# A block-sparse convolution's fourth tap stage, summed on GpSimd by additions instead of on TensorE by one-hot products

## The chip, the cores and the metric
The kernel runs on one core of one Trainium2 chip. The metric is the device time of one execution in microseconds; lower is better. A core has TensorE (PE in the profile; PEld is its weight load), VectorE (DVE), ScalarE (ACT), GpSimd (POOL) and SyncE (SP), which here only issues DMAs. GpSimd issues DMAs too, from its own instruction stream.

## What is computed
Four blocks in a row, each with a residual and a layer norm ahead of it, in float32 on an input of 2 x 512 x 256: a block-sparse convolution, a mixture of experts, an attention and the same mixture of experts again. Only the convolution is touched:

```
def _L0_attn_a_ref(x, block_values, cols, rows):      # x: (2, 512, 256), block_values: (128, 64, 64, 16)
    xb = x.reshape(batch, n_block_row, bs, t)          # 8 channel blocks of 64
    x_unfold = xb[:, cols].reshape(batch, n_blocks * bs, t)
    W = block_values.reshape(n_blocks * bs, bs, ks)
    o = jax.lax.conv_general_dilated(x_unfold, W, window_strides=(1,), padding=[(ks - 1, 0)],
            dimension_numbers=('NCH', 'OIH', 'NCH'), feature_group_count=n_blocks)
    y = jnp.zeros(...).at[:, rows].add(o.reshape(batch, n_blocks, bs, t))
    return y.reshape(batch, n_block_row * bs, t)

x = x + _L0_attn_a_ref(_layernorm(x), block_values, cols, rows)
x = x + _L0_ffn_ref(_layernorm(x), ...)
x = x + _L0_attn_b_ref(_layernorm(x), ...)
x = x + _L0_ffn_ref(_layernorm(x), ...)
```

128 weight blocks of 64 x 64 with 16 taps each (33.5 MB) are read. Blocks with the same pair (column, row) act on the same input and output channels, so the kernel first sums the weights of equal pairs (64 pairs are possible, and in this input only 16 low pairs carry weights: column and row numbers are below 4), and then multiplies the sums with the input.

## The kernel before
The 16 taps are split in eight stages of two taps. The two taps and the 64 input channels fill the 128 partitions. A stage's weights are summed over equal pairs in one of two ways.

**One-hot stages (0 to 4, `NPE = 5`).** Their weights arrive in banks, `wconv`, 512 KB each, eight for each stage, issued by SP (L247) into a ring of `RING = 6` buffers; a buffer is free again when its bank is summed (`summed`). TensorE sums a bank with the one-hot matrix of the pairs: `sum_bank`, L534, eight products with a moving size of 64, which the trace shows as 16 matmuls, as each float32 product takes two. Four PSUM banks are used in turn. ACT evicts each of them in `round_banks` (L285 for the high pairs into `full`, L286 the rounded low pairs), DVE takes the low part (`low_banks`, L397), and `sum_bank` waits for the low part of four banks earlier.

**Added stages (5 to 7, `ND = 3`).** Their weights arrive by block: `wtaps`, 16 chunks of eight blocks, 768 KB each, issued by GpSimd (L348) into three buffers `raw_d`. Before the load of chunk d (d >= 3) GpSimd waits until DVE has added chunk d - 3. DVE adds each block to the running sum `acc` of its pair, at an address from a register, in two halves (`add_block`, L421, 128 x 96: three stages of 32 columns). The pair numbers are loaded into DVE's registers eight at a time (`load_pairs`). An addition waits for all but the one before it. The additions are placed between the low parts of the banks by the table `BANK_BLOCKS`: five blocks after each bank of stages 2 and 3, then six. So DVE's order is one list: a low part that stands behind an addition waits for it.

**Products.** `products` (L545) multiplies the sums of one pair of rows with the input in three float32r products (high x high, low x high, high x low), 24 for each stage over the eight `LOW_PAIRS`. In `sum_and_convolve` the products of stage st - 1 stand between the banks of stage st, by `PACE`. `finish_products` (L568) ends a stage and raises `ws_free`, which starts at 2. `convolve_last_banks` multiplies the last one-hot stage. Then `convolve_added` multiplies the added stages, first all for row group 0, then for row group 1, after ACT (`round_sums`, L290) and DVE (`low_sums`, L405) have rounded them. ACT starts that after `ws_free` at `NPE + 1`, which is the end of stage 3's products, and after all additions. The transposes of the next layer norm (L129) stand ahead of the last piece. The first matmuls of the mixture of experts (L1131) follow the convolution's last product.

GpSimd has nothing between its loads but their waits; behind them it has a small subtraction (L157) and the powers of the next layer norm (L90).

Of the kernel before, what the change touches and what calls it, by code (L numbers as in the profile page):

```python
# [29 lines left out]
XPITCH = 272  # L30
NPE, ND = 5, 3
OB, DB, RING = 8, 8, 6

# [128 lines left out]
def conv_phase(nc, cm, pm, ps, ins, following, prefetch, first_weights):  # L162


    with ExitStack() as ctx:
        sb = lambda n, s, d: ctx.enter_context(nc.sbuf_tensor(f"cv_{n}", s, d))
        NW = NCB * NCB
        CHUNK = OB * P
        DROW = ND * BS
        NDC = NBLK // DB  # L170
# [9 lines left out]
                         .rearrange("p (w o) -> p w o", w=NLOW) for i in range(2)] for part in range(2))  # L180
        ws_hi += [sb(f"ws_hi{i}", [P, NLOW, BS], F32R)[:] for i in range(2, ND + 1)]
        ws_lo += [sb(f"ws_lo{i}", [P, NLOW, BS], F32R)[:] for i in range(2, ND + 1)]
        full = [sb(f"full{i}", [P, NW - NLOW, BS], F32) for i in range(2)]
        acc = sb("acc", [P, ND, NW, BS], F32)
        colrow = sb("colrow", [P, 2], I32)
        colrow_f = sb("colrow_f", [P, 2], F32)
# [15 lines left out]
            "zeros_ready", "ones_ready", "cr_in", "line_in", "iota_done", "const_done",  # L202
            "cr_conv", "pair_part", "pair_ready", "onehot_ready", "acc_zeroed", "added",
            "count_ready", "flag_ready", "stats_done", "moments_done", "var_ready", "rstd_ready", "xn_ready",
# [13 lines left out]
        FIRST_BLOCKS = 14  # L218
        BANK_BLOCKS = ((5,) * 8, (5,) * 8, (6, 6, 6, 6, 6, 4, 0, 0))
        PACE = (0, 0, 2, 2, 4, 4, 6, 8)  # L220
# [6 lines left out]
        def slot_of(st):  # L227
            return st % 2 if st <= NPE else st - NPE + 1

# [3 lines left out]
        def piece_of(st, r):  # L233
            return NPE * SB + r * ND + (st - NPE)

# [33 lines left out]
        def scalar(a):  # L269

            def round_input(i):
                if i == 0:
                    a.wait_ge(s["pads_ready"], 2)
                a.wait_ge(s["xn_ready"], GC * (i // 4 + 1))
                dst, src = copies(i)
                a.activation(dst(xc_hi), src, ACT.Copy).then_inc(s["xc_hi_done"], 1)

            def round_banks(st, banks=range(SB)):
                slot = st % 2
                if 0 in banks:  # L280
                    a.wait_ge(s["ws_free"], st + 1)
                for q in banks:
                    a.wait_ge(s["summed"], st * SB + q + 1)
                    sums, cols = ps[q % BANKS][:].rearrange("p (w o) -> p w o", o=OB), slice(q * OB, (q + 1) * OB)
                    a.activation(full[slot][:, :, cols], sums[:, NLOW:NW, :], ACT.Copy)  # L285
                    a.activation(ws_hi[slot][:, :, cols], sums[:, 0:NLOW, :], ACT.Copy).then_inc(s["ws_hi_done"], 1)  # L286

            def round_sums(st, r):
                e = st - NPE
                a.activation(row_part(ws_hi[slot_of(st)], r), row_part(acc[:, e, 0:NLOW, :], r), ACT.Copy)\  # L290
                 .then_inc(s["ws_hi_done"], 1)

            a.wait_ge(s["ones_ready"], 1)
            a.activation(spare[:], ones[:], ACT.Copy)
            round_banks(0, range(0, 5))
            for i in range(3):
                round_banks(0, range(5 + i, 6 + i))
                round_input(i)
            for i in range(3, 8):
                round_banks(1, range(i - 3, i - 2))  # L300
                round_input(i)
            round_banks(1, range(5, 8))
            for st in range(2, NPE):
                round_banks(st)
            a.wait_ge(s["ws_free"], NPE + 1)
            a.wait_ge(s["added"], 2 + 2 * NBLK)
            for r in range(GC // 2):
                for st in range(NPE, NST):
                    round_sums(st, r)
            first_weights["round"](a)  # L310
            a.activation(spare[:], ones[:], ACT.Silu)

        def gpsimd(g):
# [27 lines left out]
            clear_sums(range(3, ZEROED))  # L341
            g.wait_ge(s["rstd_ready"], B)
            for d in range(NDC):
                if d in (1, 2):
                    g.wait_ge(s["xc_lo_done"], 4 * d)
                if d >= 3:
                    g.wait_ge(s["added"], 2 + 2 * DB * (d - 2))
                g.dma_start(raw_d[d % 3], ins["wtaps"][d].rearrange("p (n f) -> p n f", n=DB)).then_inc(raw_d_in[d % 3], 16)  # L348
            first_weights["low"](g)
# [25 lines left out]
        def vector(v):  # L375
# [26 lines left out]
            def low_sums(st, r):  # L402
                e = st - NPE
                v.wait_ge(s["ws_hi_done"], piece_of(st, r) + 1)
                v.tensor_tensor(row_part(ws_lo[slot_of(st)], r), row_part(acc[:, e, 0:NLOW, :], r),  # L405
                                row_part(ws_hi[slot_of(st)].bitcast(F32), r), ALU.subtract).then_inc(s["ws_lo_done"], 1)
# [6 lines left out]
            def add_block(i, pairs):  # L413
                d, n = divmod(i, DB)
                if n == 0:
                    v.wait_ge(raw_d_in[d % 3], 16 * (d // 3 + 1))
                for k in range(2):
                    part = slice(k * BS // 2, (k + 1) * BS // 2)
                    dst = acc[:, :, bass.ds(pairs[n], 1), part].rearrange("p e a f -> p e (a f)")
                    src = raw_d[d % 3][:, n, :].rearrange("p (e f) -> p e f", e=ND)[:, :, part]  # L420
                    add = v.tensor_tensor(dst, dst, src, ALU.add)  # L421
                    add._wait_ge(s["added"], i * 2 + k + 1)
                    add.then_inc(s["added"], 1)
# [66 lines left out]
            for st in range(2, NPE):  # L490
                for q in range(SB):
                    low_banks(st, range(q, q + 1))
                    end = done + BANK_BLOCKS[st - 2][q]
                    edge = -(-done // DB) * DB
                    more = load_pairs(edge // DB) if edge < end else pairs
                    for i in range(done, end):
                        add_block(i, pairs if i < edge else more)
                    done, pairs = end, more
            for r in range(GC // 2):
                for st in range(NPE, NST):  # L500
                    low_sums(st, r)
# [9 lines left out]
        def tensor(t):  # L511
# [37 lines left out]
            def high_products(st):  # L549

                for c in range(NCB):
                    for r in range(GC):
                        if c >= NCB // 2 or r >= GC // 2:
# [3 lines left out]
                            else:  # L557
                                sums = acc[:, e, w:w + 2, :]
                            for x in (xc_hi, xc_lo):
# [26 lines left out]
            def convolve_added():  # L586
                for st in range(NPE, NST):
                    t.wait_ge(s["ws_lo_done"], piece_of(st, 0) + 1)
                    with t.If(flag != 0):
                        t.wait_ge(s["added"], 2 + 2 * NBLK)  # L590
                        high_products(st)
                    if st == NST - 1:
# [1440 lines left out]
```

## Time and profile before

| | us |
|---|---|
| median of 3 runs | 873.85 |
| lowest, highest | 873.17, 874.07 |
| span of the profiled execution, first to last instruction | 873.0 |
| TensorE busy, of the span | 865.5 |
| DVE busy | 501.8 |
| ACT busy | 420.0 |
| GpSimd busy | 320.0 |

The convolution takes the first 126 us of the span; the rest is the mixture of experts, the attention and the mixture of experts again. The profile counts an instruction as busy from its start to its end; matmuls overlap each other, so the mean duration of one is longer than the distance from one to the next. The chain of waits merges neighbouring instructions of one line into a piece with its start, its length and their count. The DMA share is that of the core's 16 DMA engines. "Idle before" names what released an engine that had waited; "issue" is time for which no wait is shown.

### The profile page before, as it was taken

The numbers are of one execution on the slowest core, as the hardware profiler recorded it, in microseconds if no ns is written. First come the engines' busy times: TensorE is split into PE (matmuls) and PEld (weight loads), VectorE is DVE, ScalarE is ACT, GpSimd is POOL, SyncE is SP. The second block draws the span as 40 slices with busy tenths as digits, with TensorE's granted clock in tenths as the row PEclk, the third lists the DMA queues.
The fourth block names the chain that finished last, engine by engine and source line by source line (L and its number), as shares of the span: only waits on it lengthen the run. The fifth ranks groups of instructions, "written<-read, shape, count | busy, mean of one in ns | idle before, by whom it ended". The sixth has DMA issues, their size and how long they took to land.

```text
span 873.0 us, 16737 instructions
## 1 busy us (share of the span) xinstructions
PE 865.5 (99%) x5617; PEld 773.3 (89%) x5620; DVE 501.8 (57%) x1360; ACT 420.0 (48%) x978; POOL 320.0 (37%) x293
## 2 busy tenths in 40 slices
PE   9999999999999999999999999999999999999998
PEld 7999878888888888889989998998997888888887
DVE  4777757333333338887688668768877433333334
ACT  3522416334334344776377557647746433434332
POOL 5211014556555564232121213212112556556552
PEclk9999999999999999999999999999999999999999
DMA  8999312111111102000000100000002111111111
GB/s 338 362 383 391 136 40 77 49 54 36 54 45 45 54 18 76 1 26 21 18 3 21 36 0 24 0 0 1 1 1 73 38 54 39 51 54 36 54 36 49
DMA packets 25554, 61.01 MB, mean 70 GB/s; under 512 B 3298, under 2 KB 10916, under 8 KB 25508
## 3 DMA queue, kind: packets, MB, share of 16 engines
q1 hardware_dynamic: 23204, 47.82, 16.1%
q0 software_dynamic: 2304, 12.58, 3.8%
q8 instruction: 28, 0.46, 0.2%
q14 instruction: 18, 0.15, 0.0%
HBM read 59.35 MB, written 1.05 MB: 69 GB/s over the span
## 4 chain that ended last, share of the span: by engine, by line
PE 93%; DVE 3%; ACT 1%; DMA 1%; issue 1%; POOL 0%; DVEq 0%; ACTq 0%
PE bank L1131 29%; PE bank L1655 25%; PE bank L1144 14%; PE bank L534 7%; PE bank L545 5%; PE bank L1781 4%; PE bank L1721 3%; PE bank L1157 2%; PE bank L1167 2%; DMA cv_shared<-in_wtaps 1%; PE bank L1746 1%; DVE cv_acc L421 1%; PE bank L518 1%; PE bank L1675 1%; PE bank L129 0%
## 5 line engine op out<-in xcount | busy, mean ns | idle before, releaser
L1030 DVE TENSOR_TENSOR f_h<-f_scaled,bank 128x512 f32<-128x512 f32 (+1 forms) x90 | 60.8, 676 | 179.4 <-POOL f_scaled L895 166.9
L812 ACT ACTIVATE f_h_hi<-f_h 128x512 fp32r<-128x512 f32 (+2 forms) x102 | 63.6, 624 | 186.2 <-DVE f_h L1030 186.0
L895 POOL TENSOR_TENSOR f_scaled<-f_act,f_gate_rows 128x512 f32<-128x512 f32 x80 | 102.9, 1287 | 116.3 <-ACT f_act L805 115.9
L1131 PE MATMUL bank<-f_xt_hi,f_w_lo 128*128 128x512 f32 x352 | 138.2, 393 | 0.0
L1131 PE MATMUL bank<-f_xt_hi,f_w_hi 128*128 128x512 f32 x352 | 137.8, 391 | 0.0
L1350 ACT ACTIVATE at_prob<-bank,at_sbias,at_qrs 128x512 f32<-128x512 f32 (+3 forms) x128 | 77.6, 618 | 72.6 <-DVE at_sbias L1542 72.6
L1037 DVE TENSOR_TENSOR f_h_lo<-f_h,f_h_hi 128x512 fp32r<-128x512 f32 (+2 forms) x102 | 71.8, 704 | 70.7 <-ACT f_h_hi L812 70.4
L1131 PE MATMUL bank<-f_xt_lo,f_w_hi 128*128 128x512 f32 x352 | 108.8, 390 | 0.0
L1144 PE MATMUL bank<-f_w_lo,f_h_hi 128*128 128x256 f32 (+1 forms) x352 | 99.6, 283 | 0.0
L1144 PE MATMUL bank<-f_w_hi,f_h_lo 128*128 128x256 f32 (+1 forms) x352 | 99.6, 283 | 0.0
L1144 PE MATMUL bank<-f_w_hi,f_h_hi 128*128 128x256 f32 (+1 forms) x352 | 99.3, 282 | 0.0
L805 ACT ACTIVATE f_act<-bank 128x512 f32<-128x512 f32 (+2 forms) x102 | 59.9, 589 | 52.6 <-PE bank L1131 46.4
L1413 POOL TENSOR_TENSOR at_qrs<-at_qsum,minus_half 128x4 f32<-128x4 f32 x32 | 32.8, 1025 | 137.7 <-DVE at_qsum L1503 137.7
L1131 PEld LDWEIGHTS bank<-f_xt_lo,f_w_hi 128*128 128x128 f32 x352 | 66.1, 188 | 14.4
L1131 PEld LDWEIGHTS bank<-f_xt_hi,f_w_lo 128*128 128x128 f32 x352 | 66.4, 189 | 11.1
L1131 PEld LDWEIGHTS bank<-f_xt_hi,f_w_hi 128*128 128x128 f32 x352 | 66.5, 189 | 11.0
L1144 PEld LDWEIGHTS bank<-f_w_hi,f_h_lo 128*128 128x128 f32 (+1 forms) x352 | 67.2, 191 | 3.4
L1144 PEld LDWEIGHTS bank<-f_w_hi,f_h_hi 128*128 128x128 f32 (+1 forms) x352 | 67.2, 191 | 3.3
L884 POOL TENSOR_TENSOR f_w_lo<-f_wraw,f_w_hi 128x512 fp32r<-128x512 f32 x46 | 59.5, 1293 | 25.3 <-ACT f_w_hi L791 25.3
L1144 PEld LDWEIGHTS bank<-f_w_lo,f_h_hi 128*128 128x128 f32 (+1 forms) x352 | 67.2, 191 | 0.0
L1538 DVE TENSOR_REDUCE at_smax<-bank 128x1 f32<-128x512 f32 (+3 forms) x128 | 58.8, 485 | 2.3 <-PE bank L1655 2.0
L889 POOL TENSOR_TENSOR f_w_lo<-f_wraw,f_w_hi 128x256 fp32r<-128x256 f32 x46 | 43.9, 954 | 35.1 <-ACT f_w_hi L797 35.1
(232 smaller groups left out, 2062.8 us busy)
## 6 DMA issues: line engine op xcount, KB each, us to landing
cv_raw<-in_wconv SPq DMA_DIRECT2D x26, 512.0 KB, 6.7
cv_shared<-in_wtaps POOLq DMA_DIRECT2D x16, 768.0 KB, 7.7
f_wraw<-in_w SPq DMA_DIRECT2D x42, 256.0 KB, 2.6
xn<-in_wconv SPq DMA_DIRECT2D x14, 512.0 KB, 6.5
f_wraw<-in_w SPq DMA_DIRECT2D x42, 128.0 KB, 2.5
at_wraw<-in_wqkv SPq DMA_DIRECT2D x3, 768.0 KB, 4.4
at_oraw<-in_wo SPq DMA_DIRECT2D x4, 512.0 KB, 3.5
X<-in_x_tiles SPq DMA_DIRECT2D x2, 512.0 KB, 8.0
```

Source lines behind the costliest of these rows:

```text
L534: m = t.matmul(ps[q % BANKS][:].rearrange("p (w o) -> p w o", o=OB)[:, :, o], raw[c % RING][:, o * P:(o + 1) * P], onehot[:], start=True, ...
L805: a.activation(act[half][0:rows, cols], pg[half][0:rows, cols], ACT.Silu).then_inc(s["act_done"], 1)
L812: a.activation(h_hi[slot][0:rows, cols], h_f[half][0:rows, cols], ACT.Copy).then_inc(s["h_hi_done"], 1)
L884: g.tensor_tensor(w_lo[slot][:, 0:n], raw_views(m, slot, rows)[0], w_hi[slot][:, 0:n].bitcast(F32), ALU.subtract).then_inc(s["w13_lo_done" ...
L895: g.tensor_tensor(scaled[half][:], act[half][:], gate_rows[:, half * HALF:(half + 1) * HALF], ALU.mult).then_inc(s["scaled_done"], 1)
L1030: v.tensor_tensor(h_f[half][0:rows, cols], src[half][0:rows, cols], pu[half][0:rows, cols], ALU.mult)\
L1037: v.tensor_tensor(h_lo[slot][0:rows, cols], h_f[half][0:rows, cols], h_hi[slot][0:rows, cols].bitcast(F32), ALU.subtract).then_inc(s["h_lo ...
L1131: mm = t.matmul((pg, pu)[gu][half][0:out_rows, :], w, x, start=q == 0, stop=q == 3 * KH - 1)
L1144: mm = t.matmul(bank, h[hslot][0:rows, tok], w, start=first and q == 0 and j % 2 == 0, stop=False, skip_group_check=True)
L1350: a.activation(prob[:, sl, POFF[j]:POFF[j + 1]], ps[bank][:, col:col + n], ACT.Exp, bias=sbias[:, sl, j:j + 1], scale=qrs[:, sl, j:j + 1], ...
L1538: v.tensor_reduce(smax[:, sl, j:j + 1], ps[bank][:, col:col + P * (j + 1)], AX_X, ALU.max)\
L1655: m = t.matmul(dst, l, r, start=start and q == 0, stop=stop and q == 2, skip_group_check=in_opened_bank)
```

## The change
`NPE` falls from 5 to 4, and a new `NG = 1` stands for a stage that GpSimd sums: stages 0 to 3 are one-hot sums, 4 to 6 are added on DVE as before, and stage 7 is added on GpSimd into a sum `acc_g` of its own. The chunks of `wtaps` hold four stages (16 of 1 MB), and `wconv` has 32 banks for 40. The ring of banks has five buffers for six. GpSimd's stream becomes: load chunk 0, clear `acc_g`, load chunks 1 and 2 when the input is split, and then for each chunk add eight blocks, wait for DVE's and its own additions of that chunk, and load the chunk three further. Each GpSimd addition (128 x 64) waits for the one before it. `BANK_BLOCKS` places six blocks after each bank of stages 2 and 3; what is left is added behind them. The second `full` buffer now lies on the place of the rounded sums, so that ACT's first `round_sums` waits for `ws_free` at `NPE + 2`, the end of the last one-hot stage's products; the last stage's first rounding waits for `added_g` too.

```
-NPE, ND = 5, 3
-OB, DB, RING = 8, 8, 6
+NPE, ND, NG = 4, 3, 1
+NADD = ND + NG
+OB, DB, RING = 8, 8, 5
...
-        DROW = ND * BS
+        DROW = NADD * BS
...
-        full = [sb(f"full{i}", [P, NW - NLOW, BS], F32) for i in range(2)]
+        full = [sb("full0", [P, NW - NLOW, BS], F32),
+                nc.alloc_sbuf_tensor_at("cv_full1", [P, NW - NLOW, BS], F32, offset=shared_base)]
         acc = sb("acc", [P, ND, NW, BS], F32)
+        acc_g = sb("acc_g", [P, NW, BS], F32)
...
-        BANK_BLOCKS = ((5,) * 8, (5,) * 8, (6, 6, 6, 6, 6, 4, 0, 0))
+        BANK_BLOCKS = ((6,) * 8, (6,) * 8)
...
-            a.wait_ge(s["ws_free"], NPE + 1)
+            a.wait_ge(s["ws_free"], NPE + 2)
             a.wait_ge(s["added"], 2 + 2 * NBLK)
             for r in range(GC // 2):
                 for st in range(NPE, NST):
+                    if st == NST - 1 and r == 0:
+                        a.wait_ge(s["added_g"], 1 + NBLK)
                     round_sums(st, r)
...
+            def load_blocks(d):
+                g.dma_start(raw_d[d % 3], ins["wtaps"][d].rearrange("p (n f) -> p n f", n=DB)).then_inc(raw_d_in[d % 3], 16)
+
+            def add_last_stage(d):
+                pairs = nc.values_load_multi_w_load_instructions(
+                    line_pair[0:1, d * DB:(d + 1) * DB], engines=[mybir.EngineType.Pool], min_val=0, max_val=NW - 1,
+                    skip_runtime_bounds_check_because="columns and rows are numbers of channel blocks, 0 to 7 each")[1]
+                g.wait_ge(raw_d_in[d % 3], 16 * (d // 3 + 1))
+                for n in range(DB):
+                    dst = acc_g[:, bass.ds(pairs[n], 1), :].rearrange("p a f -> p (a f)")
+                    add = g.tensor_tensor(dst, dst, raw_d[d % 3][:, n, ND * BS:], ALU.add)
+                    add._wait_ge(s["added_g"], d * DB + n + 1)
+                    add.then_inc(s["added_g"], 1)
+
+            load_blocks(0)
+            g.memset(acc_g[:], 0.0).then_inc(s["added_g"], 1)
+            for d in (1, 2):
+                g.wait_ge(s["xc_lo_done"], 4 * d)
+                load_blocks(d)
+            g.wait_ge(s["cr_conv"], 8)
             for d in range(NDC):
-                if d in (1, 2):
-                    g.wait_ge(s["xc_lo_done"], 4 * d)
-                if d >= 3:
-                    g.wait_ge(s["added"], 2 + 2 * DB * (d - 2))
-                g.dma_start(raw_d[d % 3], ins["wtaps"][d].rearrange("p (n f) -> p n f", n=DB)).then_inc(raw_d_in[d % 3], 16)
+                add_last_stage(d)
+                if d + 3 < NDC:
+                    g.wait_ge(s["added"], 2 + 2 * DB * (d + 1))
+                    g.wait_ge(s["added_g"], 1 + DB * (d + 1))
+                    load_blocks(d + 3)
...
+            while done < NBLK:
+                edge = -(-done // DB) * DB
+                if done == edge:
+                    pairs, edge = load_pairs(done // DB), done + DB
+                for i in range(done, edge):
+                    add_block(i, pairs)
+                done = edge
```

## Rows read from the trace of the kernel before

**Rows 1.** The page: span; TensorE's busy tenths and granted clock in 40 slices.
```profile
span 873.0 us, 16737 instructions
...
PE   9999999999999999999999999999999999999998
...
PEclk9999999999999999999999999999999999999999
```

**Rows 2.** Chain of waits in order of time: start, length in us, piece.
```profile
7.06 25.22 PE bank L534 x224
...
86.06 8.88 DMA cv_shared<-in_wtaps
94.94 0.03 issue
...
95.28 1.75 DVE cv_acc L421 x10
...
100.22 1.43 DVE cv_acc L421 x8
...
102.10 5.87 PE bank L545 x24
...
107.98 2.95 PE bank L545 x12
...
126.32 2.33 PE bank L1131 x10
```

**Rows 3.** Busy time of each engine by stretch, with granted clock, DMA share and GB/s.
```profile
core 0: us, PE busy (x) PEld busy (x) DVE busy (x) ACT busy (x) POOL busy (x), PEclk, DMA share, GB/s
...
41.50:61.60 20.10, 20.10 (x156) 18.79 (x155) 16.16 (x91) 5.27 (x16) 2.90 (x6) 1.00 0.96 364
61.60:81.60 20.00, 20.00 (x156) 18.78 (x155) 15.06 (x85) 5.27 (x16) 2.15 (x4) 1.00 1.02 405
81.60:101.50 19.90, 19.90 (x154) 18.63 (x153) 15.27 (x87) 5.27 (x16) 1.61 (x3) 1.00 0.67 250
```

**Rows 4.** L290 (ACT) and L405 (DVE): min, median, max in ns.
```profile
L290 ACT ACTIVATE held<-cv_acc x2: 615/622/630, 101.7 to 103.3; 128x512 fp32r<-128x512 f32 x2
...
L405 DVE TENSOR_TENSOR held<-cv_acc,held x2: 684/689/694, 102.4 to 104.2; 128x512 fp32r<-128x512 f32 x2
```

**Rows 5.** GpSimd's instructions grouped by form: count, busy us, mean ns, idle before.
```profile
L331 POOL MEMSET cv_acc<- 128x3072 f32 x4 | 10.5, 2658 | 4.7 <-DVE cv_any_high L391 3.2 <-DVE cv_shared L441 1.5
...
L912 POOL TENSOR_TENSOR f_last_lo<-f_last_raw,f_last_hi 128x512 fp32r<-128x512 f32 x2 | 2.6, 1299 | 0.0
...
L912 POOL TENSOR_TENSOR f_last_lo<-f_last_raw,f_last_hi 128x256 fp32r<-128x256 f32 x2 | 1.5, 738 | 0.0
...
L90 POOL TENSOR_TENSOR rstd<-var_eps,minus_half 128x1 f32<-128x1 f32 x2 | 1.2, 604 | 0.9 <-DVE var_eps L85 0.9
...
L317 POOL MEMSET ident<- 128x128 f32 x1 | 0.2, 204 | 0.0
```

**Rows 6.** Timeline about 105 us and 327 to 332 us: start, length, instruction.
```profile
104.82 1.29 DVE L405 TENSOR_TENSOR cv_ws_lo<-cv_acc,cv_ws_hi 128x512 fp32r<-128x512 f32 x2
104.88 0.53 ACT L153 ACTIVATE first_hi<-first_w 128x416 fp32r<-128x416 f32 x1
...
105.50 1.55 POOL L157 TENSOR_TENSOR first_lo<-first_w,first_hi 128x416 fp32r<-128x416 f32 x1 [15.03 <-ACT first_hi L153]
...
327.07 2.41 POOL L671 TENSOR_TENSOR held<-f_qkv_raw,held 128x1024 fp32r<-128x1024 f32 x1
...
328.54 1.50 DVE L1037 TENSOR_TENSOR f_h_lo<-f_h,f_h_hi 128x512 fp32r<-128x512 f32 x1 [0.70 <-ACT f_h_hi L812]
329.43 1.75 POOL L907 TENSOR_TENSOR f_scaled<-f_act,f_gate_rows 128x512 f32<-128x512 f32 x1
...
331.21 0.69 DVE L1030 TENSOR_TENSOR f_h<-f_scaled,bank 128x512 f32<-128x512 f32 x1 [1.18 <-POOL f_scaled L907]
```

**Rows 7.** L157 on GpSimd, both occurrences: min, median, max in ns.
```profile
L157 POOL TENSOR_TENSOR first_lo<-first_w,first_hi x2: 1087/1318/1549, 105.5 to 645.6; 128x416 fp32r<-128x416 f32 x2
```

**Rows 8.** DVE: groups by line to 230 us, and the longest gap in the timeline.
```profile
L421 DVE TENSOR_TENSOR cv_acc<-cv_acc,cv_shared 128x96 f32 x256 | 45.9, 251 | 11.0 <-issue 5.7 <-DMA cv_shared<-in_wtaps 4.4 <-DVE cv_acc L421 0.7
...
L397 DVE TENSOR_TENSOR held<-bank,held 128x128 fp32r<-128x128 f32 x40 | 11.3, 285 | 12.1 <-ACT held L286 11.9
...
37.45 0.76 DVE L421 TENSOR_TENSOR cv_acc<-cv_acc,cv_shared 128x96 f32 x4 [0.94 <-issue]
```

**Rows 9.** The tap loads on GpSimd: three of 16 issues, and us from issue to landing.
```profile
34.84 0.54 POOL L348 DMA_DIRECT2D cv_shared<-in_wtaps  x1 [6.44 <-DVE cv_xc_lo L447]
41.18 0.54 POOL L348 DMA_DIRECT2D cv_shared<-in_wtaps  x1 [5.80 <-DVE cv_acc L421]
...
89.93 0.54 POOL L348 DMA_DIRECT2D cv_shared<-in_wtaps  x1 [3.33 <-DVE cv_acc L421]
...
DMA to landing us min/median/max: 4.5/7.7/8.9
```

More of the change, by code:

```diff
@@ L180, in conv_phase @@
                          .rearrange("p (w o) -> p w o", w=NLOW) for i in range(2)] for part in range(2))
-        ws_hi += [sb(f"ws_hi{i}", [P, NLOW, BS], F32R)[:] for i in range(2, ND + 1)]
-        ws_lo += [sb(f"ws_lo{i}", [P, NLOW, BS], F32R)[:] for i in range(2, ND + 1)]
-        full = [sb(f"full{i}", [P, NW - NLOW, BS], F32) for i in range(2)]
+        shared_base = nc.sbuf_base
+        ws_hi += [sb(f"ws_hi{i}", [P, NLOW, BS], F32R)[:] for i in range(2, NADD)]
+        ws_lo += [sb(f"ws_lo{i}", [P, NLOW, BS], F32R)[:] for i in range(2, NADD)]
+        full = [sb("full0", [P, NW - NLOW, BS], F32),
+                nc.alloc_sbuf_tensor_at("cv_full1", [P, NW - NLOW, BS], F32, offset=shared_base)]
         acc = sb("acc", [P, ND, NW, BS], F32)
+        acc_g = sb("acc_g", [P, NW, BS], F32)
         colrow = sb("colrow", [P, 2], I32)
@@ L202, in conv_phase @@
             "zeros_ready", "ones_ready", "cr_in", "line_in", "iota_done", "const_done",
-            "cr_conv", "pair_part", "pair_ready", "onehot_ready", "acc_zeroed", "added",
+            "cr_conv", "pair_part", "pair_ready", "onehot_ready", "acc_zeroed", "added", "added_g",
             "count_ready", "flag_ready", "stats_done", "moments_done", "var_ready", "rstd_ready", "xn_ready",
@@ L227, in slot_of, with added_sums @@
         def slot_of(st):
-            return st % 2 if st <= NPE else st - NPE + 1
+            return st % 2 if st <= NPE else 1 if st == NST - 1 else st - NPE + 1
+        def added_sums(e):
+            return acc[:, e] if e < ND else acc_g[:]
         def row_part(x, r):
@@ L233, in piece_of @@
         def piece_of(st, r):
-            return NPE * SB + r * ND + (st - NPE)
+            return NPE * SB + r * NADD + (st - NPE)
         def copies(i):
@@ L289, in round_sums @@
                 e = st - NPE
-                a.activation(row_part(ws_hi[slot_of(st)], r), row_part(acc[:, e, 0:NLOW, :], r), ACT.Copy)\
+                a.activation(row_part(ws_hi[slot_of(st)], r), row_part(added_sums(e)[:, 0:NLOW, :], r), ACT.Copy)\
                  .then_inc(s["ws_hi_done"], 1)
@@ L404, in low_sums @@
                 v.wait_ge(s["ws_hi_done"], piece_of(st, r) + 1)
-                v.tensor_tensor(row_part(ws_lo[slot_of(st)], r), row_part(acc[:, e, 0:NLOW, :], r),
+                v.tensor_tensor(row_part(ws_lo[slot_of(st)], r), row_part(added_sums(e)[:, 0:NLOW, :], r),
                                 row_part(ws_hi[slot_of(st)].bitcast(F32), r), ALU.subtract).then_inc(s["ws_lo_done"], 1)
@@ L419, in add_block @@
                     dst = acc[:, :, bass.ds(pairs[n], 1), part].rearrange("p e a f -> p e (a f)")
-                    src = raw_d[d % 3][:, n, :].rearrange("p (e f) -> p e f", e=ND)[:, :, part]
+                    src = raw_d[d % 3][:, n, :].rearrange("p (e f) -> p e f", e=NADD)[:, 0:ND, part]
                     add = v.tensor_tensor(dst, dst, src, ALU.add)
@@ L557, in high_products @@
                             else:
-                                sums = acc[:, e, w:w + 2, :]
+                                sums = added_sums(e)[:, w:w + 2, :]
                             for x in (xc_hi, xc_lo):
@@ L590, in convolve_added @@
                         t.wait_ge(s["added"], 2 + 2 * NBLK)
+                        t.wait_ge(s["added_g"], 1 + NBLK)
                         high_products(st)
@@ L2003 @@
         "wtaps": a["attn_a_block_values"].reshape(NBLK // DB, DB, BS, BS, NST, 2)[:, :, :, :, NPE:]
-                 .transpose(0, 5, 3, 1, 4, 2).reshape(NBLK // DB, P, DB * ND * BS),
+                 .transpose(0, 5, 3, 1, 4, 2).reshape(NBLK // DB, P, DB * NADD * BS),
         "w13": routed13.transpose(1, 2, 0, 3, 4).reshape(2, NRT, P, KH, P).transpose(1, 4, 3, 0, 2)
```

## The prediction
> **What bounds the kernel now.** I read the page first: TensorE is busy over the whole span and its granted clock stays in the top tenth of full speed, so only a shorter or longer chain on TensorE moves the time [rows 1]. The chain of waits in order of time then shows which part belongs to the convolution. From 7 us on it is TensorE alone: one-hot sums (L534) and products (L545) back to back. 224 one-hot matmuls take 25.22 us, 0.1126 us each, so the 128 of one stage take 14.4 us; the 24 product matmuls of a stage take 5.9 us [rows 2]. The busy times by stretch confirm it: three stages of 20 us, each filled by TensorE (14.4 + 5.9 = 20.3) [rows 3].
>
> The reader must see in the same rows that TensorE isn't the only full resource. The share of the DMA engines is 0.96 to 1.02 until 81.6 us and DVE is busy for 15 to 16 of 20 us [rows 3]. At the end of the one-hot work three things finish within 7 us: the next to last block load lands at 94.9, the last addition on DVE ends at 101.65, and TensorE starts the products of the last one-hot stage at 102.1 [rows 2]. At 107.98 it begins the products of the three added stages and at 126.32 the FFN starts: 18.34 us [rows 2]. What follows is work of the FFN and attention that the change doesn't touch. So I forecast the moment at which the FFN's first products start, and add its shift to the median.
>
> **What is removed.** One one-hot stage: 14.4 us of TensorE, eight bank evictions on ACT and eight low parts on DVE (0.285 us each [rows 8]). With nothing in its place TensorE would be through the convolution 14.4 us earlier. But the bytes are the same: 4 MB of bank loads become 4 MB in the tap loads (16 of 1 MB for 16 of 768 KB). DMA was full to about 95 us, so the last chunk can't land much before 95 to 97 us. The change moves the bound from TensorE to the loads and the additions; the 14.4 us aren't the gain, they are cover.
>
> **What is added at the end.** Four added stages are multiplied after the additions instead of three: 18.34 + 5.9 = 24.2 us from their start to the FFN. Rounding their first piece takes an ACT pass of 0.62 and a DVE pass of 0.69 us [rows 4], 1.3 us ahead of it. Before, both ran under the products of the last one-hot stage; now the second `full` buffer lies under the rounded sums, so ACT waits for those products to end (`ws_free` at `NPE + 2`), and the 1.3 us stand in the open. The GpSimd sum is needed only 3 x 12 matmuls (3 x 2.95 = 8.8 us [rows 2]) later, so its own end isn't what the chain waits for. Ring five for six: the 512 KB loads still have four or more in flight; I cost it at nothing, covered by the full DMA. Zeroing `acc_g` is 4096 elements against 3072 in 2.66 us [rows 5], 3.5 us, and lies in GpSimd's wait of 6.4 us ahead of its third load [rows 9]: nothing.
>
> **What GpSimd costs.** This is the term that decides. 128 additions of 128 x 64 run in a row, each waiting for the one before. The trace has no such instruction. The nearest rows are GpSimd subtractions of 512 and 256 columns: 1.299 and 0.738 us [rows 5], so 2.19 ns a column and 0.177 us fixed: 0.32 us for 64 columns. To that comes the hand-over between two dependent ones: from ACT's end (105.41) to GpSimd's start (105.50) is 0.09 us [rows 6]. So 0.41 us if nothing is in the way. Bounds: below, a clearing of 128 columns takes 0.204; above, a power of one element takes 0.604 fixed [rows 5], which gives 0.604 + 0.14 + 0.09 = 0.83.
>
> Something is in the way. In the timeline a DVE subtraction with both inputs in SBUF starts at 328.54 while a GpSimd one runs until 329.48; it takes 1.50 us where its like take 0.69, and ends 0.56 after GpSimd's end. The GpSimd one that starts at 329.43 takes 1.75 instead of 1.29: it waits for DVE in turn [rows 6]. At 105.50 again: 1.55 us beside DVE, 1.087 alone [rows 6, 7]. DVE's block additions have both inputs in SBUF. They come every 0.175 us (ten in 1.75 [rows 2]) and last 0.251 [rows 8], each reading for about 0.10 us: from 96 to 512 columns the time grows from 0.251 to 0.69, 1.06 ns a column. GpSimd reads for 64 x 2.19 ns = 0.14, say 0.15 us of its 0.32. So by estimate a GpSimd addition waits about 0.05 (0.46 in all) and costs DVE 0.15.
> The Trainium skill speaks against the change here: by "SBUF — State Buffer", section "Who interferes with whom", a VectorE instruction with two SBUF inputs contends with a GpSimd instruction that reads SBUF, and the other side blocks fully. The rows above agree. Without that rule the sum would go by 0.41 us and no loss on DVE, which is the rival "light" below.
>
> Per chunk of eight blocks GpSimd then needs 8 x 0.46 = 3.7 us, the DMA issue of 0.54 [rows 9], and the loading of eight pair numbers with the waits about it. On DVE that loading leaves 15 gaps, 5.7 us together, 0.38 each (the release "issue" [rows 8]); the trace has none on GpSimd, and I take 0.6 (bounds: 0.2, if the loading runs under the DMA issue, and 0.94, the longest gap on DVE [rows 8]). That is 4.8 us. DVE needs 16 x 0.175 = 2.8, 8 x 0.15 = 1.2 blocked, 0.35 for low banks, 0.35 for pair numbers: 4.7 us. They are coupled both ways: `load_blocks(d + 3)` stands in GpSimd's own stream and waits for `added` and `added_g`, so behind it are queued GpSimd's next eight additions and its next load, and DVE waits for that load two chunks later; DVE's low banks are queued behind its additions, so TensorE is slowed with it. Before, a chunk took (89.93 - 41.18) / 12 = 4.06 us [rows 9]. I take 4.8.
>
> **The sum.** DVE's first chunk ends 1.1 us later than in [rows 9] (its blocking), 42.3. The last load is issued after chunk 12: 42.3 + 12 x 4.8 = 99.9. It lands in 5 us (4.5 was the fastest of 768 KB, 7.7 the median beside the bank loads [rows 9], which are over by then): 104.9. DVE's 16 additions, partly blocked, 3.5: 108.4. Rounding 1.3: 109.7. Products of four stages 24.2: 133.9 against 126.3, so +7.6. TensorE's last one-hot products (from about 100.5 to 106.4, as the last low bank is queued behind chunk 12) are under this. The profiled execution has a span of 873.0, 0.85 below the median; the shift carries over: 873.85 + 7.75 = 881.6. In general: 873.85 + 12 x chunk - 49.85.
>
> **Rivals.**
> 1. Light: additions take 0.41 us or less and hardly meet. Then the loads bound as before. Chunk 15 could be added by 97.7 + 2.9 = 100.6; 1.3 and 24.2 more give 126.1, -0.2 us: 873.7. Only if the larger loads also keep DMA at the 405 GB/s of its best stage instead of 364 [rows 3] does the last landing come up to 4 us earlier: 869.9. This is not slower than before. It decides where a chunk takes under 4.3 us. For it: 0.32 comes from firm rows, and of the hand-over only 0.03 us may remain on one engine, as from GpSimd's end (331.18) to DVE's start (331.21) [rows 6]. Against it: 8 x 0.41 + 1.1 is already 4.4 us, with no conflict at all.
> 2. Heavy: small register-addressed additions cost GpSimd more than the line through wide ones says, or the two engines wait for each other more often: 0.6 us, 5.9 us a chunk, +21: 894.8. For it: all the wide rows are over 0.7 us and say little on fixed cost; the power's 0.604.
> 3. The clock: TensorE waits some 3 us before the added stages, and about 1 us in each bank of stage 3. Rows show the granted clock in its top tenth all along [rows 1], but also no such wait. At 1.2 GHz instead of 2.4 a stage's products take 5.9 us more; one to two stages: 887.5 to 893. The Trainium skill, "TensorE: Matmul & The Clock Gate", Part 1, says that an idle array falls to 1.2 GHz; whether these pauses do it no row here can show.
> 4. That the additions run elsewhere or the stage isn't moved: no place for it in the diff; under 0.01.
>
> **How the numbers follow.** Forecast (chunk 4.4 to 5.4 us, 876.8 to 888.8): 0.47. Light: 0.29, of it 0.10 faster by over 0.2% (below 872.1) and 0.19 within it. Heavy 0.16, clock 0.08. A measurement of this kernel tells 0.2%, 1.75 us, from no change. So slower 0.71. The range 872.0 to 893.5 takes in most of light and the near part of heavy; some 0.1 lie below and 0.1 above.
>
> **What would show it.** The sum of GpSimd in the profile after: 128 instructions of about 0.32 to 0.4 us, starts 0.46 apart; the DVE ones longer than 0.251 on average; tap loads issued 4.8 us apart; DMA share below 0.9 from 45 us on; the first product of the added stages at 109.7, 24.2 us before the FFN. The prediction is wrong if the loads are 4.1 us apart (light) or near 6 (heavy), if the added stages begin right behind the last one-hot products, or if the granted clock falls.

## The result and the profile after

The changed kernel takes 891.87 us (median of 4 runs, 891.11 to 893.11) against 873.81 before: the ratio is 1.0205, 95% interval 1.0191 to 1.0218. It is slower by 18.1 us, where 7.75 were forecast. Its profiled execution has a span of 890.7 us, 17.7 more than in [rows 1].

The head of its page is read first. TensorE is busy for nearly the same time in a longer span, although 14.4 us of its work are gone (matmuls at a lower clock take longer); GpSimd is busy for 375 us instead of 320, and the clock row is no longer all nines: it is lower in four of the second to sixth slices, in the convolution.

```profile
span 890.7 us, 16728 instructions
...
PE 866.0 (97%) x5488; PEld 771.8 (87%) x5491; DVE 509.0 (57%) x1354; ACT 416.0 (47%) x964; POOL 374.8 (42%) x422
...
PE   9998679999999999999999999999999999999998
...
PEclk9898779999999999999999999999999999999999
```

The chain of waits from the last tap load to the FFN (start, length, piece) answers to [rows 2]. The FFN's first matmul comes at 143.98 for 126.32, so all 17.7 us are lost ahead of it and nothing after it.

```profile
106.92 5.03 DMA cv_shared<-in_wtaps
...
112.74 0.35 DVE cv_acc L452 x2
113.09 0.11 issue
113.20 0.35 DVE cv_acc L452 x2
...
115.05 0.74 DVE cv_acc L452 x3
115.86 0.64 ACT held L299
116.53 0.70 DVE held L436
117.23 0.50 issue
117.73 11.15 PE bank L583 x36
128.93 11.30 PE bank L583 x48
140.23 0.87 PE bank L130 x8
141.10 2.88 PE bank L583 x24
143.98 2.09 PE bank L1170 x9
```

The same stretches as in [rows 3], and those about the added stages (the last three numbers are granted clock, DMA share and GB/s). TensorE has gaps and the clock is down. The DMA engines are full until 81.6 us, as before; but where before they had little left to move behind 95 us, they now run at 0.57 to 0.63 until 110 us: the loads wait for the additions.

```profile
41.50:61.60 20.10, 20.10 (x156) 19.51 (x154) 15.41 (x78) 4.13 (x14) 11.60 (x28) 0.92 0.90 321
61.60:81.60 20.00, 18.84 (x121) 17.41 (x121) 14.73 (x69) 3.96 (x12) 14.67 (x39) 0.83 1.02 406
81.60:101.50 19.90, 15.79 (x76) 13.63 (x76) 16.51 (x84) 2.63 (x8) 15.61 (x34) 0.77 0.63 229
101.50:110.00 8.50, 5.14 (x21) 3.90 (x19) 4.06 (x21) 0.00 (x0) 6.11 (x17) 0.90 0.57 182
110.00:120.00 10.00, 2.27 (x5) 1.84 (x6) 7.37 (x26) 2.00 (x4) 7.66 (x19) 0.50 0.15 60
120.00:130.00 10.00, 10.00 (x39) 7.84 (x38) 4.12 (x7) 4.31 (x8) 1.47 (x1) 0.84 0.02 5
```

GpSimd's timeline answers to [rows 9]. The fourth load goes out at 44.88 instead of 41.18 and the last at 106.92 instead of 89.93: 12 chunks of 5.17 us. One chunk stands out: the eight additions from 95.75 take 5.99 us where the others take 3.3 to 3.9 (4.3 the last, which runs beside the rounding).

```profile
36.40 3.27 POOL L364 TENSOR_TENSOR cv_acc_g<-cv_acc_g,cv_shared 128x64 f32 x8 [0.45 <-issue]
44.88 0.58 POOL L355 DMA_DIRECT2D cv_shared<-in_wtaps  x1 [5.21 <-DVE cv_acc L452]
...
51.43 0.58 POOL L355 DMA_DIRECT2D cv_shared<-in_wtaps  x1 [1.77 <-DVE cv_acc L452]
52.17 3.68 POOL L364 TENSOR_TENSOR cv_acc_g<-cv_acc_g,cv_shared 128x64 f32 x8 [0.16 <-issue]
...
95.01 0.58 POOL L355 DMA_DIRECT2D cv_shared<-in_wtaps  x1 [0.56 <-DVE cv_acc L452]
95.75 5.99 POOL L364 TENSOR_TENSOR cv_acc_g<-cv_acc_g,cv_shared 128x64 f32 x8 [0.17 <-issue]
102.30 0.58 POOL L355 DMA_DIRECT2D cv_shared<-in_wtaps  x1 [0.56 <-DVE cv_acc L452]
...
106.92 0.58 POOL L355 DMA_DIRECT2D cv_shared<-in_wtaps  x1 [0.56 <-POOL cv_acc_g L364]
```

### The profile page after: what moved, and what is told of

Same layout as the page of the kernel before. It is cut to its first block, busy times and chain, and to the rows that moved or that the text cites. A ratio compares the mean times of both kernels' runs of the same rounds, so it can differ in the third digit from the quotient of the medians.

```text
span 890.7 us, 16728 instructions
## 1 busy us (share of the span) xinstructions
PE 866.0 (97%) x5488; PEld 771.8 (87%) x5491; DVE 509.0 (57%) x1354; ACT 416.0 (47%) x964; POOL 374.8 (42%) x422
## 4 chain that ended last, share of the span: by engine, by line
PE 84%; POOL 6%; DVE 3%; issue 3%; POOLq 1%; ACT 1%; DMA 1%; DVEq 0%; ACTq 0%
PE bank L1170 28%; PE bank L1694 24%; PE bank L1183 14%; POOL cv_acc_g L364 5%; PE bank L1820 4%; PE bank L583 3%; PE bank L1760 3%; PE bank L1196 2%; PE bank L1206 2%; PE bank L1785 1%; POOLq L358 1%; PE bank L572 1%; PE bank L556 1%; DMA cv_shared<-in_wtaps 1%; POOLq L364 1%
## 5 line engine op out<-in xcount | busy, mean ns | idle before, releaser
L1170 PEld LDWEIGHTS bank<-f_xt_lo,f_w_hi 128*128 128x128 f32 x352 | 66.1, 188 | 14.4
L1170 PEld LDWEIGHTS bank<-f_xt_hi,f_w_lo 128*128 128x128 f32 x352 | 66.4, 189 | 11.1
L452 DVE TENSOR_TENSOR cv_acc<-cv_acc,cv_shared 128x96 f32 x256 | 53.5, 279 | 16.1 <-DMA cv_shared<-in_wtaps 12.0
```

What stands on the lines that cost most here:

```text
L1170: mm = t.matmul((pg, pu)[gu][half][0:out_rows, :], w, x, start=q == 0, stop=q == 3 * KH - 1)
```

## The experiments

The theory after the result had three parts: the ring of five banks lets TensorE run dry at 36 us; DVE's and GpSimd's additions hold each other up; TensorE's clock falls after its waits. The rivals were that the pace of the chunks is GpSimd's own length plus its in-order loads, and that the larger loads bind whatever the engines do. Times of runs of before beside them were 873.9 to 874.3.

**1. The ring alone, from both sides.** The changed kernel with six banks; the sixth lies on a rounded-sum buffer that is free until the additions are over:

```
-OB, DB, RING = 8, 8, 5
+OB, DB, RING = 8, 8, 6
...
-        raw += [sb(f"raw{i}", [P, CHUNK], F32)[:] for i in range(2, RING)]
+        raw += [sb(f"raw{i}", [P, CHUNK], F32)[:] for i in range(2, RING - 1)]
...
         shared_base = nc.sbuf_base
+        raw += [nc.alloc_sbuf_tensor_at("cv_raw5", [P, CHUNK], F32, offset=shared_base + (NW - NLOW) * BS * 4)[:]]
```

> The changed kernel with a ring of six banks again (the sixth buffer lies on a rounded-sum buffer that is free until the additions are over). Theory (the smaller ring lets TensorE run dry at 36 us; it waits 1.26 us for a bank, its granted clock falls to 0.50 for some 6 us, DVE's first chunk is late): no wait for a bank near 36 us, granted clock 1.0 from 30 to 45 us, the fourth tap load issued near 42 instead of 44.9 us, time 2 to 4 us shorter than 891.9, so 888 to 890. Rival (the 1 MB loads take the bandwidth whatever the ring, or the late chunk is made up later by GpSimd's pace): the wait stays, or the time stays within 1 us of 891.9.

Measured: 886.64 us (885.61 to 887.75), 5.2 less than the changed kernel. The wait is gone. In the timeline of TensorE after the change the bank is missing at 36.3, and the 16 matmuls behind the wait take 3.46 us instead of 2.00:

```profile
34.27 2.00 PE L572 MATMUL bank<-cv_onehot,cv_raw 128*128 128x64 f32 x16
37.53 3.46 PE L572 MATMUL bank<-cv_onehot,xn 128*128 128x64 f32 x16 [1.26 <-DMA xn<-in_wconv]
```

With five (first) and with six banks (second), the stretch behind it by engine:

```profile
38.00:42.00 4.00, 4.00 (x20) 4.00 (x21) 1.18 (x5) 0.66 (x2) 1.44 (x4) 0.50 1.04 426
```
```profile
38.00:42.00 4.00, 4.00 (x38) 3.96 (x36) 3.87 (x23) 0.00 (x0) 1.45 (x4) 1.00 1.02 421
```

At half clock TensorE does half the matmuls (20 for 38), DVE waits for the last low parts of stage 1, which stand in its order among the first additions, and so the fourth load goes out at 44.88 instead of 41.09. The gain is above the expected 2 to 4 us, as the second chunk was late too (51.43 for 46.45, so 5.0 us after two chunks). About 1 us more in the profiles can come from the chunk of 7.29 us (95.01 to 102.30), which is told of below; the longest of a_ring6 took 5.97.

The other side, the kernel before with a ring of five (`OB, DB, RING = 8, 8, 5`) and nothing else:

> The kernel before with a ring of five instead of six banks and nothing else. Theory (five buffers are too few beside the tap loads): TensorE waits for a bank once or more between 24 and 45 us and the time is 1 to 4 us over 873.8. Rival (it takes the 1 MB tap loads for that, 768 KB ones leave the banks enough): within 0.5 us of 873.8.

Measured: 876.98 us (10 runs, 874.84 to 879.54), ratio 1.0028 (1.0016 to 1.0041). Here too TensorE waits for banks (three times, 0.3 to 1.0 us) and the clock is at 0.57 from 38 to 42 us. In its profile (an execution of 878.26 us) the chain then waits for a last bank, issued at 90.02 and landed at 100.67, and the FFN starts 3.4 us late. So the smaller ring costs on its own, 768 KB loads or 1 MB. Its time scatters over 4.7 us where before scatters over 1.2; that the ring runs dry more often in some executions than in others is likely, but only one was traced.

**2. GpSimd's additions left out**, first with the ring of five, then with six:

```
                 g.wait_ge(raw_d_in[d % 3], 16 * (d // 3 + 1))
-                for n in range(DB):
-                    dst = acc_g[:, bass.ds(pairs[n], 1), :].rearrange("p a f -> p (a f)")
-                    add = g.tensor_tensor(dst, dst, raw_d[d % 3][:, n, ND * BS:], ALU.add)
-                    add._wait_ge(s["added_g"], d * DB + n + 1)
-                    add.then_inc(s["added_g"], 1)
+                g.sem_inc(s["added_g"], DB)
```

> The changed kernel with GpSimd's 128 additions left out (its sum stays zero, so stage 7 is missing in the output); the loads, their waits and the loading of the pair numbers stay. Theory (GpSimd's additions set the pace of the tap loads, 5.17 us a chunk): the chunks fall to 4.2 to 4.4 us, the DVE additions back to 0.175 us apart, the last load is issued near 94 us and the added stages begin near 103; time 874 to 878. Rival (the pace is set by DVE's order with its waits for TensorE's banks, or by the loads): chunks stay at 4.8 us or more, time over 883.

> a_ring6 with GpSimd's additions left out (stage 7's sum is zero in the output); loads, waits and pair numbers stay. Theory (without GpSimd's work the loads and DVE bind; what is left over the kernel before is the exposed rounding, the fourth added stage against a last landing that can't come earlier, and the clock after the wait): chunks 4.1 to 4.3 us, added stages from 103 to 105, time 874.5 to 878. Rival (the ring was only the first of several stalls that the larger loads bring): 880 or more.

Measured: 881.64 us (a single execution) with five and 876.74 (876.23 to 877.68) with six. With six banks the last load goes out at 91.05, 4.12 us a chunk, and the added stages begin at 102.73. With five the chunks took 4.25 us as expected, but the time missed its range: the fourth load was late again (45.07), which the expectation had forgotten. So the additions on GpSimd cost 9.9 us (886.64 - 876.74), the ring 5, and 2.9 us remain that neither explains. The same loads at 4.12 us a chunk also settle the rival of the larger loads: they don't set the pace of 4.95.

**3. The same length on GpSimd without reading.** Is it GpSimd's time or what it shares? Each addition becomes a clearing of 256 columns, chained and counted in the same way:

```
-                    dst = acc_g[:, bass.ds(pairs[n], 1), :].rearrange("p a f -> p (a f)")
-                    add = g.tensor_tensor(dst, dst, raw_d[d % 3][:, n, ND * BS:], ALU.add)
+                    dst = acc_g.rearrange("p (w a) f -> p w (a f)", a=4)[:, (d * DB + n) % 16, :]
+                    add = g.memset(dst, 0.0)
```

> a_ring6 (the changed kernel, ring of six) with each of GpSimd's 128 additions replaced by a clearing of 256 columns of its sum, which takes about as long (0.31 us) and is chained and counted in the same way, but reads nothing from SBUF; stage 7's sum is zero in the output. Theory (the two engines take turns at the port through which GpSimd and DVE's second input read): GpSimd's steps come 0.40 us apart for 0.46, DVE's additions go back to 0.175 us apart without long ones, chunks take 4.5 instead of 4.95 us and the added stages begin 5 us sooner: 880 to 883 against 886.6. Rival (no port is shared to a degree that counts; the chunk time is GpSimd's own length plus issue and pair numbers): chunks stay at 4.9, time within 1 us of 886.6.

Measured: 876.76 us (875.49 to 877.96), the time of no work on GpSimd at all and below the expected 880 to 883: the chunks took 4.24 us (41.75 to 92.67 in twelve), where 4.5 were expected. GpSimd was busy 311 ns at each step, as long as an undisturbed addition (318 at the median in run 4). So most of the 9.9 us isn't its occupied time; what costs is that its additions read SBUF beside DVE's. The rows of both additions, minimum, median and maximum in ns, with the clearings (first) and with the additions (second):

```profile
L453 DVE TENSOR_TENSOR cv_acc<-cv_acc,cv_shared x256: 245/252/261, 38.0 to 100.6; 128x96 f32 x128
...
L365 POOL MEMSET cv_acc_g<- x128: 311/311/333, 35.9 to 101.7; 128x256 f32 x128
```
```profile
L453 DVE TENSOR_TENSOR cv_acc<-cv_acc,cv_shared x256: 243/248/424, 37.2 to 109.3; 128x96 f32 x128
...
L365 POOL TENSOR_TENSOR cv_acc_g<-cv_acc_g,cv_shared x128: 311/382/1722, 35.6 to 112.8; 128x64 f32 x128
```

This is what the Trainium skill says in "SBUF — State Buffer", section "Who interferes with whom": a VectorE instruction with two SBUF inputs contends with a GpSimd instruction that reads SBUF, and not with one that only writes it. The trace agrees on both halves: DVE's longest addition took 424 ns beside the additions and 261 beside the clearings. The clearing isn't a perfect stand-in: its steps come 0.37 us apart and not 0.395, and without an address from a register the 0.17 us ahead of each chunk falls away, some 0.4 us a chunk. The next run bounds what that hides.

**4. DVE's additions left out**, GpSimd's kept:

```
-                for k in range(2):
...
-                    add = v.tensor_tensor(dst, dst, src, ALU.add)
-                    add._wait_ge(s["added"], i * 2 + k + 1)
-                    add.then_inc(s["added"], 1)
+                v.sem_inc(s["added"], 2)
```

> a_ring6 with DVE's 256 additions left out (stages 4 to 6 missing in the output) and GpSimd's kept: GpSimd works alone. Theory (alone GpSimd needs 8 x 0.395 for the additions and 1.3 for its own end, the issue and the pair numbers, 4.46 us a chunk, and the rest of the 4.95 is the sharing): tap loads 4.5 us apart, no addition on GpSimd over 0.45 us, added stages from about 102 as the last load lands near 98.5; 876 to 879. Rival (GpSimd's own pace is the whole of it): loads 4.9 us apart, 883 or more.

Measured: 875.30 us (874.04 to 875.85), just under the expected 876 to 879. Alone, GpSimd needs 4.39 us a chunk from 50 us on, near the expected 4.46: eight additions in 3.09, then 0.56 for its own last end, 0.58 for the issue, 0.17 ahead of the first addition.

```profile
50.10 3.10 POOL L365 TENSOR_TENSOR cv_acc_g<-cv_acc_g,cv_shared 128x64 f32 x8 [0.16 <-issue]
53.75 0.58 POOL L356 DMA_DIRECT2D cv_shared<-in_wtaps  x1 [0.56 <-POOL cv_acc_g L365]
54.49 3.09 POOL L365 TENSOR_TENSOR cv_acc_g<-cv_acc_g,cv_shared 128x64 f32 x8 [0.17 <-issue]
58.13 0.58 POOL L356 DMA_DIRECT2D cv_shared<-in_wtaps  x1 [0.56 <-POOL cv_acc_g L365]
```

With both at work (a_ring6) it is (100.54 - 41.09) / 12 = 4.95 us. So of the 9.9 us the sharing makes 12 x 0.56 = 6.7 in the chunks, 0.9 in DVE's last 16 additions (3.8 us for 2.9) and some 1.2 in the clock of the added stages (26.4 us for 25.2). What is left, about 1 us, can be GpSimd's own pace: alone it needs 4.39 us a chunk, the clearings 4.24, so at most 12 x 0.15 = 1.8 us that run 3 put down to the sharing. By this estimate the sharing is 8 to 9.9 us.

**5. The loads taken out of GpSimd's stream.** SyncE issues the tap loads between its bank loads, with the same two waits; GpSimd only adds:

```
+            after_bank = {14: (0,), 17: (1,), 20: (2,), 21: (3,), 23: (4,), 24: (5,), 26: (6,), 28: (7,), 29: (8,),
+                          31: range(9, NDC)}
             for c in range(6, NPE * SB):
                 bank_blocks(c)
+                for d in after_bank.get(c, ()):
...
+                    if d >= 3:
+                        sp.wait_ge(s["added"], 2 + 2 * DB * (d - 2))
+                        sp.wait_ge(s["added_g"], 1 + DB * (d - 2))
+                    load_blocks(d)
```

> a_ring6 with the tap loads issued by SyncE between its bank loads instead of by GpSimd; GpSimd only adds and no longer waits for DVE. The result is whole. Theory (the sharing of the port is most of the loss, GpSimd's in-order loads a smaller part): GpSimd saves 0.56 + 0.58 us a chunk, but DVE's additions stay 0.21 us apart and chunks take 4.3 to 4.6 us; 879 to 884 against 886.6. Rival 1 (the in-order loads are the loss): near 877. Rival 2 (one queue for both kinds of loads holds the banks back behind the additions): 887 or more.

Measured: 881.06 us (880.42 to 881.93), 5.6 less than a_ring6, inside the expected range, with chunks of 4.33 us (40.99 to 93 in twelve). But the theory with it had the loads in GpSimd's stream as the smaller part, and they are the larger: 5.6 of the 9.9 us are gone, while the additions still meet. The sharing costs 9.9 us only where GpSimd's additions, its waits and its next load stand in one order; without that it costs about 4.3 (881.06 - 876.74; no run has these loads without the additions). Now DVE binds: its 256 additions take more than ever, 296 ns on average for 251 in [rows 8], as GpSimd no longer pauses to issue loads, and its waits for loads are down to 3.7 us from 10.6:

```profile
L454 DVE TENSOR_TENSOR cv_acc<-cv_acc,cv_shared 128x96 f32 x256 | 57.9, 296 | 7.4 <-DMA cv_shared<-in_wtaps 3.7 <-issue 1.6 <-DVE cv_acc L454 0.9
```

**6. The fourth stage on DVE**, nothing added on GpSimd, whose additions are left out as in 2:

```
-        acc = sb("acc", [P, ND, NW, BS], F32)
-        acc_g = sb("acc_g", [P, NW, BS], F32)
+        acc = sb("acc", [P, NADD, NW, BS], F32)
+        acc_g = acc[:, ND]
...
-                    src = raw_d[d % 3][:, n, :].rearrange("p (e f) -> p e f", e=NADD)[:, 0:ND, part]
+                    src = raw_d[d % 3][:, n, :].rearrange("p (e f) -> p e f", e=NADD)[:, :, part]
```

> a_ring6 with the fourth added stage summed on DVE too (256 additions of 128 x 128 in place of 128 x 96) and nothing added on GpSimd, which only loads. The result is whole. Theory (GpSimd's in-order additions and the turns at the port cost more than the same columns on DVE): additions 0.21 us apart, 8.5 us more on DVE, chunks 4.3 to 4.5 us, added stages from 106; time 877 to 881, well under a_ring6. Rival (DVE is the bound, and GpSimd did take load off it): 885 or more.

Measured: 881.21 us (880.28 to 881.78), 5.4 less than with GpSimd's help, just above the expected 877 to 881. GpSimd takes 32 of 128 columns off DVE, which cost 4.5 us there (881.21 - 876.74) and 9.9 on GpSimd.

**7. The clock.** TensorE gets products of zeros, 0.216 us each, in time in which it waits; at the end of the one-hot work:

```
             convolve_last_banks()
+            for _ in range(34):
+                t.matmul(ps[7][:], zeros[:, 0:P], zeros[:], start=False, stop=False)
             convolve_added()
```

The first two kernels have 45 there, and 3 after each bank of stages 2 and 3 and ahead of the last one-hot products.

> The changed kernel with idle work for TensorE, products of zeros added to an accumulator: 3 after each bank of stages 2 and 3, 3 ahead of the last one-hot products and 45 (9.6 us) ahead of the added stages, all in time that it waits anyway. Theory (the granted clock of 0.50 after waits costs 2 us in the added stages and slows stage 3): granted clock 1.0 behind 120 us, the four added stages in 24.2 us instead of 26.25, time 2 to 4 us shorter, 888 to 890. Rival (the clock costs nothing that isn't waited for anyway, or the added work pushes the last products back): within 1 us of 891.9 or longer.

> a_ring6 with the idle work for TensorE of a_fill (3 products of zeros after each bank of stages 2 and 3, 48 at the end). Theory (with the ring's stall gone the clock is the next loss: 0.50 to 0.76 in the added stages and 0.66 to 0.85 in stage 3): added stages in 24.2 us instead of 26.4, granted clock 1.0 all through, time 883.5 to 885 against 886.6. Rival (the fillers delay what they should speed, or the clock costs nothing): 886 or more.

> a_ring6 with 34 products of zeros (7.4 us) between the last one-hot products and the added stages, in a wait of 7.9 us, and no others. Theory (a_r6_fill got nothing because its 45 ran 1.8 us past the end of the wait; the clock itself costs 2.2 us in the added stages): added stages at 24.2 us, time 884 to 885. Rival (the clock after the wait costs nothing that can be won back): 886 or more.

Measured: 891.37 (886.70 to 893.14), 886.39 (885.21 to 886.70) and 885.73 (885.38 to 885.95) us, against 891.87, 886.64 and 886.64. The clock did what was expected. In a_r6_fill it is 1.00 in the added stages, which then take 23.5 us (113.31 to 136.81) where a_ring6 took 26.4 (111.57 to 137.98). But the fillers ran until 113.31 while the first sums were ready at about 111.5, so 1.2 us were left in the profiles and 0.25 in the medians. With the number cut to 34, all ahead of the added stages, 0.9 us are left. All three expectations were missed. The lower clock of a_ring6 during stage 3 (0.66 to 0.85 from 60 to 100 us) costs nothing: a_r6_fill has 1.00 there until 90 us, and its last tap load goes out at 100.97 for 100.54, as TensorE waits there for DVE anyway. (The first of the three is not conclusive: its six executions scatter over 6.4 us, and the traced one is the fastest, 886.70.)

None of the versions beats the kernel before. Even those that leave additions out, with six banks, stay at 875.3 to 876.8.

## Why the prediction was off

The direction, the place (ahead of the FFN's first matmul) and the mechanism of GpSimd's and DVE's additions were right, the size wasn't: +17.7 us in the profile for +7.6. By the steps of the sum:

| step | forecast | in the profile after |
|---|---|---|
| fourth load issued (end of DVE's first chunk) | 42.3 | 44.88 |
| twelve chunks | 12 x 4.8 = 57.6 | 12 x 5.17 = 62.04 |
| last load to landing | 5 | 5.03 |
| DVE's last 16 additions | 3.5 | 3.8 (to 115.77) |
| rounding | 1.3 | 1.96 |
| four added stages | 24.2 | 26.25 |
| FFN starts | 133.9 | 143.98 |

**The ring of five: costed at nothing, worth 5 us.** This step failed. The prediction counted buffers in flight and named the full DMA as cover. A full DMA is no cover for a ring but what empties it. The banks issued between 24 and 36 us landed in 9.7 and 9.9 us (medians of both kinds of buffer) after the change:

```profile
cv_raw<-in_wconv SPq DMA_DIRECT2D x4, 512.0 KB, 9.7
xn<-in_wconv SPq DMA_DIRECT2D x2, 512.0 KB, 9.9
```

Before it was 6.4 and 6.8. TensorE summed a bank in 1.8 us at this place, where products stand between few of the banks. The bank that was missing was issued at 27.5 us, when its buffer was free, and TensorE wanted it 9.0 us after that buffer had been summed (27.3 to 36.3). A sixth buffer gives it 1.8 us more, 10.8. a_ring6 won back 5.2 us and b_ring5 lost 2.7. With six banks the time of 886.64 lies between the 876.8 and 888.8 that the prediction gave its own case, so without this step its size would have been near. The ring accounts for the late first chunk (2.6 us against the forecast, 3.8 against a_ring6) and for most of the second (6.55 us, 44.88 to 51.43).

**The pace of the chunks: right term, a little short.** With six banks it was 4.95 us for 4.8 forecast. The parts came out near: an undisturbed addition 0.31 us (0.32), its step 0.395 us (0.41), what stands about the issue 1.3 us (1.14). Wrong was the even alternation. Mostly the two did alternate: GpSimd's median is 382 ns, and DVE's go in pairs each 0.46 us. But where DVE's additions run in an unbroken row, GpSimd may get no turn for a while. In the timeline of the kernel after (first its row over all additions), GpSimd gets through three additions in 3.76 us, while DVE adds 12 in 2.11 and 12 in 2.10, its pace without any sharing:

```profile
L364 POOL TENSOR_TENSOR cv_acc_g<-cv_acc_g,cv_shared x128: 308/382/2143, 36.4 to 119.3; 128x64 f32 x128
...
94.60 2.11 DVE L452 TENSOR_TENSOR cv_acc<-cv_acc,cv_shared 128x96 f32 x12
95.01 0.58 POOL L355 DMA_DIRECT2D cv_shared<-in_wtaps  x1 [0.56 <-DVE cv_acc L452]
95.75 3.76 POOL L364 TENSOR_TENSOR cv_acc_g<-cv_acc_g,cv_shared 128x64 f32 x3 [0.17 <-issue]
96.64 0.28 DVE L428 TENSOR_TENSOR held<-bank,held 128x128 fp32r<-128x128 f32 x1
96.84 2.10 DVE L452 TENSOR_TENSOR cv_acc<-cv_acc,cv_shared 128x96 f32 x12
```

That chunk took 7.29 us. The rival "heavy" named waits for each other as one of its two causes; what it hadn't is that they come in fits, on one side only. Such chunks stand in other traces too, at other times (5.97 us from 65.22 in a_ring6).

**The clock: the rival happened.** It was given 0.08, as a case of its own; in fact it came on top of the forecast's case. The granted clock was 0.50 from 110 to 120 us and the added stages took 2.05 us more. Its forecast place, the wait ahead of the added stages, was right, but the wait was 11.1 us long, not 3. The prediction named a falling clock as a sign that it is wrong, and the sign came. That 891.87 lies in this rival's 887.5 to 893 is luck: the clock makes 2.05 of the 10 us of error. The rule of the Trainium skill that was cited with it ("TensorE: Matmul & The Clock Gate", Part 1, an idle array falls to 1.2 GHz) agrees with the trace: 0.50 is that level.

**Rounding.** 1.96 for 1.3 us: 0.09 ahead of ACT's pass and 0.50 between DVE's pass and the first product had no row in the sum. The prediction blamed the `full` buffer under the rounded sums for the exposure. The trace says otherwise: the last one-hot products ended at 106.6 and the additions at 115.8, so the wait at `ws_free` was long over. The place of that buffer cost nothing.

**The rival "light" gives the floor.** It did not happen, but it put the FFN at 126.1 without any conflict; a_r6_memset has it at 128.09 and a_r6_noaddg at 127.95, 1.85 us behind the rival's time in the second. 1.0 us of that is the clock (25.2 us from 102.73 on for 24.2), 0.6 the rounding (1.95 us for 1.3) and 0.2 the additions (to 100.78 for 100.6). So what the prediction said first held: 14.4 us of TensorE's work removed were cover and no gain, as the bytes and the last additions stand where they stood. Of the 10 us of error, the ring is 2.6 + 1.75 (the first chunk, and the second at 6.55 for 4.8), the clock 2.05, the chunk without turns 2.5 (7.29 for 4.8); rounding and small differences are the rest. The clock was taken as an alternative when here it is a consequence of the long wait. A sign of the prediction failed as well: the DMA share was to be below 0.9 from 45 us on, and was 1.02 from 61.6 to 81.6.

In short: of 18.1 us, 5.2 are the ring (shown) and 9.9 GpSimd's additions (shown). By the estimate above 8 us or more of the 9.9 are the sharing of SBUF reads between GpSimd and DVE, with the clock loss that it brings (shown by equally long instructions that read nothing), and the sharing costs so much only with the loads in GpSimd's own order: with these on SyncE 4.3 are left. The last 2.9 are what a fourth added stage costs with no sharing. In the profiles it is 1.6 (127.95 for 126.32), about 1.0 of it the clock. The difference is that the traced execution of before was a long one: in all later runs the span is 1.8 us below the execution's own time, so its 873.0 belongs to some 874.8 and not to the median, as the prediction took it. What gives one side a long run of turns was not tried.

## What to carry to other kernels

Handing small two-input additions from DVE to GpSimd isn't relief while DVE does the same: price each by what it takes from the other, and look in the trace for a pair that overlapped before trusting a sum of durations. If the helper engine issues loads that others wait for, its delays go into every one of them; another engine's queue can carry the loads. A ring is as deep as the landing time under full DMA asks at the place where its reader is fastest, not on average. And a wait on TensorE is to be priced with its clock: the work behind it may run at half speed, so the wait and the slow stretch go in the same case.

## What the runs showed of the hardware

- A wait of 1.26 us on TensorE (36.27 to 37.53) was followed by a granted clock of 0.50 from 38 to 42 us; the 16 matmuls behind it took 3.46 us instead of 2.00. The same came in b_ring5, where waits of 0.3 to 1.0 us stood ahead of 0.57. No wait of TensorE in these stretches was longer.
- Two engines that hold each other up needn't alternate: one GpSimd addition of 0.31 us took up to 2.14 us beside a row of DVE additions that lost nothing.
- Writes of GpSimd alone disturbed DVE not at all: 252 ns median, 261 at most, beside 128 clearings; in the kernel before, with nothing beside them, 251 and 260.
